# Second FFN GEMM of a transformer layer on plain float32 operands, with the query and key projections spread over more units

## The reference

```
q = x @ wq + x @ Aq @ Bq * 4;  k = x @ wk;  v = x @ wv + x @ Av @ Bv * 4      # heads of 16
q, k = rope(q), rope(k)
a = softmax(causal(q @ k.T / 4)) @ v;   x = layernorm(x + a @ wo)
h = gelu(butterfly(x @ W_exp + b_exp, up_weights) + up_bias)                  # 1024 wide
y = butterfly(h, down_weights) @ W_con + b_con + down_bias;   x = layernorm(x + y)
```

## Time and profile before

| | |
|---|---|
| median of 3 runs | 1371.78 us (1365.69 to 1373.66) |
| the profiled execution | 1372.62 us, its span 1370.9 us, mean granted clock of TensorE 0.923 |
| loop turns | begin about every 77 us |

### The profile page before, as it was taken

How to read it: one execution, slowest core, us unless ns; L and a number is a source line. 1 busy time by engine, 2 the same in 40 slices (tenths; PEclk the granted TensorE clock), 3 DMA queues, 4 the chain that set the end, 5 groups by cost and what they waited for, 6 DMA issues and landing times.

```text
span 1370.9 us, 27389 instructions
## 1 busy us (share of the span) xinstructions
PE 1154.4 (84%) x8328; PEld 811.3 (59%) x8328; DVE 834.9 (61%) x1896; ACT 757.5 (55%) x1259; POOL 630.8 (46%) x648
## 2 busy tenths in 40 slices
PE   4466789797889889898989899897989899899775
PEld 3334456665566566665666576665656576666464
DVE  5587766565647657475757667575757666575332
ACT  1156557465465657466564647466564647466612
POOL 2121424546355454637355454637355454635333
PEclk9667789999999999999999999999999999899999
DMA  5734454534445353544546353544546353542110
GB/s 184 191 119 111 132 125 112 150 102 140 105 147 139 118 148 94 169 118 135 118 147 144 114 148 94 167 119 135 118 147 146 112 148 94 170 117 60 49 40 31
DMA packets 94982, 169.88 MB, mean 124 GB/s; under 512 B 14872, under 2 KB 36120, under 8 KB 94944
## 3 DMA queue, kind: packets, MB, share of 16 engines
q1 hardware_dynamic: 93888, 166.53, 44.4%
q10 hardware_dynamic: 832, 1.83, 0.4%
q0 software_dynamic: 224, 1.04, 0.2%
HBM read 92.28 MB, written 77.07 MB: 124 GB/s over the span
## 4 chain that ended last, share of the span: by engine, by line
PE 53%; issue 14%; DVE 11%; POOL 11%; DMA 6%; ACT 4%; POOLq 0%; SPq 0%; DVEq 0%; ACTq 0%
PE ps_m L532 19%; PE ps_m L671 10%; PE ps_m L640 9%; PE ps_t L612 6%; POOL x1T_lo L1040 5%; DMA x_res<-in_x 4%; PE ps_s L574 3%; PE ps_s L600 3%; DVE m_raw L876 3%; POOL rot L1030 3%; DVE m_raw L871 2%; POOL pT L1020 2%; ACT pT L745 2%; DMA qk_scr<-rot 1%; PE ps_m L649 1%
## 5 line engine op out<-in xcount | busy, mean ns | idle before, releaser
L876 DVE TENSOR_REDUCE m_raw<-ps_s 128x1 f32<-128x512 f32 (+2 forms) x768 | 346.2, 506 | 278.8 <-PE ps_s L600 276.6
L745 ACT ACTIVATE pT<-ps_t 128x512 f32<-128x512 f32 x640 | 345.3, 593 | 148.4 <-PE ps_t L612 146.8
L1020 POOL TENSOR_SCALAR_AFFINE_SELECT pT<-pT 128x512 f32<-128x512 f32 (+1 forms) x320 | 175.4, 548 | 399.7 <-ACT pT L745 399.7
L1040 POOL TENSOR_TENSOR x1T_lo<-gact,x1T_hi 128x512 fp32r<-128x512 f32 x128 | 163.0, 1278 | 73.4 <-ACT x1T_hi L796 73.1
L574 PE MATMUL ps_s<-k_st,q_st 48*128 48x512 f32 (+3 forms) x1024 | 138.8, 329 | 43.9 <-DVE m_raw L876 22.6
L640 PE MATMUL ps_m<-pT,v_aug 128*32 128x512 f32 (+3 forms) x2048 | 170.8, 479 | 4.5 <-POOL pT L1020 3.3
L612 PE MATMUL ps_t<-q_st,k_st 50*128 50x512 f32 (+3 forms) x1024 | 173.0, 396 | 0.0
L671 PE MATMUL ps_m<-w_hi,x1T_hi 128*128 128x256 f32 x512 | 100.9, 324 | 67.4 <-POOL x1T_lo L1040 67.3
L612 PEld LDWEIGHTS ps_t<-q_st,k_st 50*128 50x128 f32 x1024 | 83.5, 190 | 90.2 <-issue 75.7
L574 PEld LDWEIGHTS ps_s<-k_st,q_st 48*128 48x128 f32 x1024 | 98.0, 195 | 56.3 <-DVE m_raw L876 32.2
L671 PEld LDWEIGHTS ps_m<-w_hi,x1T_hi 128*128 128x128 f32 x512 | 77.7, 212 | 77.8 <-POOL x1T_lo L1040 65.7
(11 more groups left out here) (119 smaller groups left out, 1984.7 us busy)
## 6 DMA issues: line engine op xcount, KB each, us to landing
qk_scr<-rot_hi SPq DMA_DIRECT2D x64, 512.0 KB, 3.6
q_st<-qk_scr SPq DMA_DIRECT2D x128, 192.0 KB, 4.7
k_st<-qk_scr SPq DMA_DIRECT2D x128, 192.0 KB, 5.1
qk_scr<-rot SPq DMA_DIRECT2D x32, 512.0 KB, 3.2
o_scr<-o_raw SPq DMA_DIRECT2D x64, 256.0 KB, 2.1
r_b<-in_xT SPq DMA_DIRECT2D x17, 512.0 KB, 6.5
o_c<-o_scr SPq DMA_DIRECT2D x32, 256.0 KB
r_b<-r_scr SPq DMA_DIRECT2D x32, 256.0 KB
```

The costliest lines, as they stand in the source:

```text
L745: act.activation(pT[:, g % 2, slot, half * T:(half + 1) * T], ps_t[:, ST_BANK[2 * n + r], :], ACT.Exp, scale=SCALE).then_inc(exp_done, 1)
L876: ins = dve.tensor_reduce(m_raw[:, r, u // 2, qt:qt + 1], ps_s[:, r, off:off + (qt + 1) * P], AX.X, ALU.max, negate=True)
L1020: pool.affine_select(out=v, in_=v, compare_op=ALU.is_ge, fill=0.0, base=0, pattern=pattern, channel_multiplier=-1).then_inc(mask_done, 1)
L1040: pool.tensor_tensor(g_lo[:, half, :, :], gact[:, NHT // 2 * half:NHT // 2 * (half + 1), tile * P:(tile + 1) * P], g_hi[:, half, :, :].bit ...
```

## The change

The second GEMM uses `gact` (the GELU's output) and one float32 `w2` as they are, with one product for each hidden tile in place of three matmuls. `w2_hi`, `w2_lo`, `g_hi`, `g_lo`, the steps GHI and GLO and their semaphores go; W2 waits for `gelu_done` of half 0, W2B for that of half 1, and DM writes `w2` only. `gact` is read by PE directly.

The tables change too. QK piece 0 of batch i+2 stands in unit 19's front, so behind S of unit 18, QK 1 of batch i+1 in unit 0, QK 2 in unit 2, QK 3 in unit 4. W1 pieces 6 and 7 move from unit 19 into units 0 and 1 of the next turn, and GE of half 1 from unit 0 to unit 1. W2 and W2B of tiles 0 and 1 stand together behind S of units 4 and 5, and tile 2 behind S of unit 6. RAW moves behind S of its unit, RB(i,0) ahead, XRES(i-1,0), LNS, HIGH, LOW, QKH and QKL later. The maxima's transpose MT is emptied by VectorE, no longer by ScalarE.

On PE, `QK3 MT1 | S10 PV3 | S11 W2-0 | S12 W2B-0 W2-1 | S13 W2B-1 | S14 W2-2 W2B-2 MT2` becomes `QK2 MT1 | S10 PV3 | S11 QK3 | S12 W2-0 W2B-0 | S13 W2-1 W2B-1 | S14 W2-2 W2B-2 MT2`. The diff, with the declarations left out:

```diff
@@ -67,15 +67,18 @@
 
 
 
-    qk, w2, wo, v, xt, w1 = i + 1, i - 2, i - 1, i + 1, i - 1, i - 1
-    front = {0: [("QK", qk, 0), ("QK", qk, 1)], 1: [("QK", qk, 2)], 2: [("QK", qk, 3), ("MT", i, 1)],
-             4: [("W2", w2, 0)], 5: [("W2", w2, 1)], 6: [("W2B", w2, 1)], 7: [("W2B", w2, 2), ("MT", i, 2)],
-             9: [("W2", w2, 3)], 10: [("WO", wo, 0)], 11: [("WO", wo, 1)], 12: [("V", v, 0), ("MT", i, 3)],
-             14: [("XT", xt, 0), ("XT", xt, 1)], 15: [("W1", w1, 0)], 16: [("W1", w1, 2)],
-             17: [("W1", w1, 4), ("MT", i + 1, 0)], 19: [("W1", w1, 6)],
-             3: [("PV", i - 1, 3)], 8: [("PV", i, 0)], 13: [("PV", i, 1)], 18: [("PV", i, 2)]}
-    back = {4: [("W2B", w2, 0)], 6: [("W2", w2, 2)], 9: [("W2B", w2, 3)], 14: [("V", v, 1)],
-            15: [("W1", w1, 1)], 16: [("W1", w1, 3)], 17: [("W1", w1, 5)], 19: [("W1", w1, 7)]}
+    front = {0: [("QK", i + 1, 1)], 1: [("W1", i - 2, 7)], 2: [("QK", i + 1, 2), ("MT", i, 1)],
+             3: [("PV", i - 1, 3)], 4: [("QK", i + 1, 3)], 5: [("W2B", i - 2, 0)], 6: [("W2B", i - 2, 1)],
+             7: [("W2B", i - 2, 2), ("MT", i, 2)], 8: [("PV", i, 0)], 9: [("W2", i - 2, 3)],
+             10: [("WO", i - 1, 0)], 11: [("WO", i - 1, 1)], 12: [("V", i + 1, 0), ("MT", i, 3)],
+             13: [("PV", i, 1)], 14: [("XT", i - 1, 0), ("XT", i - 1, 1)], 15: [("W1", i - 1, 0)],
+             16: [("W1", i - 1, 2)], 17: [("W1", i - 1, 4), ("MT", i + 1, 0)], 18: [("PV", i, 2)],
+             19: [("QK", i + 2, 0)]}
+    back = {0: [("W1", i - 2, 6)], 4: [("W2", i - 2, 0)], 5: [("W2", i - 2, 1)], 6: [("W2", i - 2, 2)],
+            9: [("W2B", i - 2, 3)], 14: [("V", i + 1, 1)], 15: [("W1", i - 1, 1)], 16: [("W1", i - 1, 3)],
+            17: [("W1", i - 1, 5)]}
+    if static and i == -1:
+        front[0] = [("QK", 0, 0), ("QK", 0, 1)]
     after = {"MT": "MOUT", "W2B": "W2E", "PV": "OE"}
 
     def gemms(table, t):
@@ -83,37 +86,27 @@
             put(kind, b, n)
             if kind in after:
                 put(after[kind], b, n)
-            if kind == "PV":
-                put("RAW", b, n)
-
-    def halves(b, n):
-        put("GHI", b, n)
-        put("GLO", b, n)
 
     for t in range(NU):
 
         if t == 0:
             put("FILL", i, 3)
-        if t == 2:
-            halves(i - 2, 0)
         for at, b, n in ((3, i, 1), (8, i, 2), (13, i, 3), (18, i + 1, 0)):
             if t == at:
                 put("MROW", b, n)
-        if t == 3:
-            halves(i - 2, 1)
         if t == 4:
             put("VC", i)
         if t == 5:
+            put("QKL", i + 1, 0)
             put("SMOC", i - 1, 1)
         if t == 6:
             put("RCP", i - 1, 1)
             put("REC", i - 1, 1)
         if t == 7:
-            put("XRES", i - 1, 0)
             put("RB", i - 1, 1)
-            put("LNS", i - 2, 2)
         if t == 8:
             put("ON", i - 1, 1)
+            put("LNS", i - 2, 2)
         if t == 10:
             put("LNS", i - 2, 3)
         if t == 12:
@@ -132,42 +125,38 @@
         if t == 17:
             put("LNB", i - 2, 2)
         if t == 18:
+            put("RB", i, 0)
             put("LNB", i - 2, 3)
 
         gemms(front, t)
-        for at, n in ((4, 2), (5, 4), (6, 5), (7, 7)):
-            if t == at:
-                halves(i - 2, n)
-        if t == 11:
-            put("LNS", i - 1, 0)
 
         put("ST", i, t)
         put("S", *((i, t + LEAD) if t + LEAD < NU else (i + 1, t + LEAD - NU)))
 
         gemms(back, t)
-        for at, n in ((4, 3), (6, 6)):
-            if t == at:
-                halves(i - 2, n)
 
         if t == 17:
             put("GE", i - 1, 0)
-        if t == 0:
+        if t == 1:
             put("GE", i - 2, 1)
         if t == 0:
             put("ROPE", i + 1, 0)
-        if t == 1:
+        if t == 2:
             put("HIGH", i + 1, 0)
+            put("LOW", i + 1, 0)
+        if t == 3:
             put("QKH", i + 1, 0)
-            put("LOW", i + 1, 0)
-        if t == 2:
-            put("QKL", i + 1, 0)
+        for at, b, n in ((3, i - 1, 3), (8, i, 0), (13, i, 1), (18, i, 2)):
+            if t == at:
+                put("RAW", b, n)
+        if t == 4:
             put("ROPE", i + 1, 1)
-        if t == 3:
+        if t == 6:
             put("HIGH", i + 1, 1)
             put("QKH", i + 1, 1)
-        if t == 5:
             put("LOW", i + 1, 1)
-        if t == 6:
+        if t == 7:
+            put("XRES", i - 1, 0)
             put("QKL", i + 1, 1)
         if t == 8:
             put("FILL", i + 1, 0)
@@ -184,7 +174,6 @@
         if t == 16:
             put("XLO", i + 2, 0, B + 1)
         if t == 18:
-            put("RB", i, 0)
             put("OUT", i - 2)
         if t == 19:
             put("ON", i, 0)
@@ -665,14 +649,12 @@
                 elif kind in ("W2", "W2B"):
 
                     half = int(kind == "W2B")
-                    pe.wait_ge(glo_done, NHT * b + 2 * n + half + 1)
-                    for j, (a, c) in enumerate(((0, 0), (0, 1), (1, 0))):
-                        for k in range(NHT // 2):
-                            mm = pe.matmul(pm[:, 0:D], (g_hi, g_lo)[a][:, half, k, :],
-                                           (w2_hi, w2_lo)[c][:, NHT // 2 * half + k, :],
-                                           start=(half + j + k == 0),
-                                           stop=(half == 1 and j == 2 and k == NHT // 2 - 1))
-                    mm.then_inc((w2_half, done["W2"])[half], 1)
+                    pe.wait_ge(gelu_done, 2 * b + half + 1)
+                    for k in range(NHT // 2 * half, NHT // 2 * (half + 1)):
+                        mm = pe.matmul(pm[:, 0:D], gact[:, k, n * P:(n + 1) * P], w2[:, k, :],
+                                       start=(k == 0), stop=(k == NHT - 1))
+                    if half:
+                        mm.then_inc(done["W2"], 1)
                 elif kind == "UM":
 
                     if n == 0:
@@ -785,17 +762,7 @@
                     act.activation(tile_up[n], pm[:, 0:D], ACT.Copy).then_inc(evac["UM"], 1)
                 elif kind == "DM":
                     act.wait_ge(done["DM"], n + 1)
-                    act.activation(w2_hi[:, n, :], pm[:, 0:D], ACT.Copy).then_inc(w2h_done, 1)
-                elif kind == "GHI":
-                    tile, half = n // 2, n % 2
-                    if tile:
-
-                        act.wait_ge((w2_half, done["W2"])[half], NT * b + tile)
-                    else:
-                        act.wait_ge(gelu_done, 2 * b + half + 1)
-                    act.activation(g_hi[:, half, :, :],
-                                   gact[:, NHT // 2 * half:NHT // 2 * (half + 1), tile * P:(tile + 1) * P],
-                                   ACT.Copy).then_inc(ghi_done, 1)
+                    act.activation(w2[:, n, :], pm[:, 0:D], ACT.Copy).then_inc(evac["DM"], 1)
                 elif kind in ("XU", "XD"):
 
                     k = int(kind == "XD")
@@ -894,6 +861,10 @@
                     dve.tensor_tensor(rope_in[:, a[0], :], pm, cs[:, a[1], :], ALU.mult)
                     dve.tensor_tensor(rope_in[:, c[0], :], pm, cs[:, c[1], :], ALU.mult)\
                        .then_inc(evac["QK"], 1)
+                elif kind == "MT":
+                    dve.wait_ge(done["MT"], NG * b + n + 1)
+                    wait(dve, mrow_out, DMA * (NG * b + n))
+                    dve.tensor_copy(m_row[:, :], pm[0:NM * GH * NT, 0:P]).then_inc(evac["MT"], 1)
                 elif kind == "XT":
                     dve.wait_ge(x1h_done, 2 * b + n + 1)
                     dve.tensor_tensor(x1T_lo[:, n, :], pm, x1T_hi[:, n, :].bitcast(FP32),
```

More of the change, by code:

```diff
@@ L178, in steps @@
         if t == 11:
+            put("LNS", i - 1, 0)
             put("XTL", i + 2, 0, B + 1)
@@ L279, in layer @@
             tmp_x = before_w2.enter_context(nc.sbuf_tensor("tmp_x", [P, 2, D], FP32))
-        w2_hi = sb("w2_hi", [P, NHT, D], F32R)
-        w2_lo = sb("w2_lo", [P, NHT, D], F32R)
+        w2 = sb("w2", [P, NHT, D])
         ga = gact[:, :, :].rearrange("p a c -> p (a c)")
@@ L346, in layer @@
         w_hi, w_lo = sem("w_hi"), sem("w_lo")
[L347 to L351, removed]
+        w1h_done = sem("w1_hi_done")
         pool_c = sem("pool_c")
@@ L763, in one @@
                        .then_inc(vcopy, 1)
[L764 to L768, removed]
                 elif kind == "HIGH":
@@ L917, in one @@
                        .then_inc(evac_w1[1], 1)
-                elif kind == "DM":
-                    dve.wait_ge(w2h_done, n + 1)
-                    dve.tensor_tensor(w2_lo[:, n, :], pm[:, 0:D], w2_hi[:, n, :].bitcast(FP32),
-                                      ALU.subtract).then_inc(evac["DM"], 1)
                 elif kind == "W2E":
@@ L1036, in one @@
                         .then_inc(on_done, 1)
-                elif kind == "GLO":
-                    tile, half = n // 2, n % 2
-                    pool.wait_ge(ghi_done, NHT * b + n + 1)
```

(5 more changed lines are left out.)

## The result

The changed kernel takes 1290.84 us (median of four executions, 1289.61 to 1295.52), the kernel before beside it on the same chip 1368.74 us (1365.09 to 1373.66). The ratio is 0.9435, 95% interval 0.9391 to 0.9479: 5.6% faster. The forecast of 1270 us was 21 us too low, inside its range. The profiled execution took 1295.52 us with a span of 1293.8 us, so 77 us of span are gone where the sum had 102.

What follows compares the result with a forecast made beforehand. PE's instruction stream was taken to set the turn: 77.0 - 9.2 + 1.9 + 0.65 = 70.3 us, taken as 70.0. 13 turns save 91 us, with start and end 102 us together: 1270 us, range 1243 to 1310.

Steps and rivals of the forecast that it cites:

- Part 1: GELU parts go: PE's GpSimd waits at the second GEMM and the slow stretch behind them vanish, 5.6 us a turn.
- Part 2: Second GEMM in plain float32: its eight halves cost PE 1.9 us more a turn, 2.5 at most.
- the walk: Step-by-step timing of a turn from S(i,6): WO starts at 39.1 us, before 46.2, so a turn of 69.9.
- Part 3: QK pieces set apart: at MT(i,1) 2.20 + 1.4 us of wait and slow stretch go, 0.65 come.
- Part 4: MT emptied by VectorE: three of four a turn cost nothing; unit 12's gains 0.1 us at most, none counted.
- the wait moves from MT3 to XT: Unit 12: MT(i,3) loses its 0.92 us wait, XT waits on VectorE's 0.3 us longer chain; gain 0.1 at most.
- Part 5: SP's queue reordered: maxima transfers and RB(i,0) earlier, XRES(i-1,0) and RB(i-1,1) later, at no cost, with 3.5 us of cover.
- Turns 15 and 16: W1 pieces 6 and 7 (3.0 us) fill PE's 3.25 us masks wait; plain halves cost 1.9; about 4 us gained.
- A: The waits move: about 2 us at MT1 or W2(i-2,0)'s bank plus slow stretch, 3.6 us a turn, 1317 us; chance 0.13.
- B: Slower: a wait ahead of unit 4 leaves GEMM 2 at half clock, up to 13.8 us a turn, 1449 us; chance 0.05.
- C: GEMM's waits pass to the next in line, 5.6 us a turn stay, 1343 us; chance 0.04, plus 0.02 shared with B.
- D: More gain: the 0.65 us, XT chain and three boundary waits vanish, 1.5 us a turn, 1250 us or under; chance 0.10.

Runs made afterwards that it cites:

- e7: The kernel before with only the second GEMM in plain float32, plus XRES(i-1,1) issued ahead of FILL(i+1,0): 1316.94 us, ratio 0.9603.
- e2: The kernel before, its own order of pieces kept, with only the second GEMM changed to plain float32: 1329.25 us, ratio 0.9709.
- e4: The changed kernel with MT emptied by ScalarE as before the change: 1287.16 us, ratio 0.9409.
- e10: e9 with MT emptied by ScalarE as before the change: 1260.79 us, ratio 0.9196.
- e9: e5 with the statistics LNS(i-1,0) moved to unit 10: 1263.08 us, ratio 0.9220.
- e1: The changed kernel with SP issuing XRES(i-1,1) ahead of FILL(i+1,0): 1268.91 us, ratio 0.9271.
- e5: The changed kernel with the rotation's stores (HIGH, QKH, LOW, QKL) issued earlier, FILL(i+1,0) left in place: 1266.24 us, ratio 0.9227.
- e11: e5 with half of GEMM 2's products left out, so the output is not the layer's: 1241.45 us, ratio 0.9069.
- e8: The changed kernel with half of GEMM 2's products left out, so the output is not the layer's: 1273.35 us, ratio 0.9315.

## Why the prediction was right or wrong

**Part 1, right.** No wait on the GELU's parts is left but 1.1 us in the last turn, and e7 gives the forecast's turn for the plain GEMM, 73.3 us.

**Part 2, right in size, and the rule did not decide.** Eight products are one group of 16 instructions in 3.46 to 3.67 us (665.84 above), 1.73 to 1.83 a half, 0.216 us an instruction. The estimate made with the Trainium skill ("FP8 and Floating Point Precision", TensorE Precision Notes: four passes for true FP32) was 1295 us, nearer to 1290.84 than the forecast. Its four passes agree with the trace, 0.432 us for a product, but its reason for the time isn't the one found. All eight halves of a turn stand ahead of WO, and there the walk holds: 39.4 us where 39.1 was forecast, so the 1.6 us a turn that the estimate adds aren't there. What is missing lies behind WO, and that it is 1.6 us a turn too is chance.

**Part 3, right.** MT1's wait went from 2.20 to 0.39 us, WO stands at 39.4 us, and in e2, which keeps the old order, MT1 still waits 2.2 us in every turn of the loop.

**Part 4, right in cost, wrong in what comes last.** e4 shows the cost of nothing, and e10 against e9 does so again. The step "the wait moves from MT3 to XT" failed: XT waits 0.32 us and MT3 1.79, because the sum ahead of `m_pad` waits for `x_res`.

**Part 5 is the step that failed.** It priced the steps that moved on SP's queue at nothing, with XRES(i-1,0) and RB among them. FILL(i+1,0) and XRES(i-1,1) did not move in the list, and I did not price them. But W2E(i-2,3), which releases the load, now comes 7 us sooner after S6, while the store of the keys' low half, which FILL needs, goes out only 2 us sooner (680.86 - 647.62 = 33.2 us after S6, before 721.36 - 686.21 = 35.2) and lands in 4.5 us instead of 3.1. The FILLs come 5 us sooner. So four FILL loads of 768 KB together, 2 us clear of the load before, now stand right ahead of it. It takes 1.5 us longer to land, and WO to XT gets 14.05 - 12.46 = 1.6 us longer a turn, 21 us in 13 turns. e1 and e5 take the cause away in two ways, and e5 has the turn that was forecast, 69.8. The four loads ahead are what slows it: e1 leaves the stores where they were, has FILL loads right behind the load and none right ahead, and there it lands in 2.9 to 3.2 us.

The prediction's opening says by the earlier trace rows that no DMA queue is near its limit; these rows have no DMA in them. The page has the busiest queue at 44.4% of its engines' time, which is a mean over the span and says nothing of these 2 us.

**Turns 15 and 16: 4 us of gain forecast, 7.4 lost.** Up to the last W1 they are 7.4 us longer, 6.8 of these up to the PV that the earlier trace rows show at 1297.29. The W1 pieces that moved across the boundary are 3.0 of the 6.8, and the plain GEMM 2.2. The pieces were to fit into a wait, but the waits up to that PV sum to 9.9 us, before to 10.0. About 2 us are W1 pieces that run at the lower clock behind waits: the first two matmuls of the one at 1204.38 take 1.19 us, before 0.70 in the same place. PV behind a wait takes 3.92 us in this turn, before 4.50, so PV isn't the difference. PE's timeline:

```profile
1153.13 0.80 PE L558 MATMUL ps_s<-k_st,q_st 48*128 48x384 f32 x4 [1.33 <-DVE m_raw L843]
...
1196.17 0.30 PE L616 MATMUL ps_m<-ident,m_pad 128*128 128x128 f32 x1 [1.78 <-DVE m_pad L854]
...
1196.82 3.92 PE L624 MATMUL ps_m<-pT,v_aug 128*32 128x512 f32 x32
...
1204.38 1.19 PE L516 MATMUL ps_m<-x1T_hi,w_hi 128*128 128x512 f32 x2 [1.62 <-DVE x1T_lo L870]
...
1224.88 3.97 PE L624 MATMUL ps_m<-pT,v_aug 128*32 128x512 f32 x32 [2.04 <-POOL pT L987]
```

The wait of 3.25 us into which the pieces were to fit became 2.04 us here, and the waits ahead of it grew by as much, from 6.8 to 7.8 us. I moved two pieces and did not walk these turns.

**The last turn, right.** From the last W1 to the end of the GEMM took 15.2 us, 5.3 less than before, forecast 5:

```profile
1270.65 1.89 PE L654 MATMUL ps_m<-w,gact 128*128 128x256 f32 x8
...
1273.66 12.35 PE L654 MATMUL ps_m<-w,gact 128*128 128x256 f32 x56 [1.12 <-ACT gact L795]
```

**Summed up.** Turns -1 to 1 gained 3.6 us (forecast 2), turns 2 to 14 gained 75.6 (91), turns 15 to the end lost 2.1 (9 gained): 77 of 102. The 13 turns sum to 932.5 us, before to 1008.1, where the forecast had 910 and 13 x 77.0 = 1001. The load's 21 us are in the 22 by which they are too long. But they had been 7 us longer than 1001 before (turn 3 took 81.6), and those hide a third of the load's share in the gain. So it is chance that the total was off by 21 us too, and that e1 and e5 come to 1269 and 1266 us, near the 1270 of the forecast: e5 gains some 9 us more in its 13 turns and 6 more ahead of them than was forecast, and loses 3 at the end where 9 were to be gained. **The rivals:** A had the right kind of event, a wait that takes the place of the one removed, but put it at MT1 or at W2(i-2,0), and priced it at 3.6 us a turn; it came at MT3 with 1.6. B did not come, the clock is 0.99. C is refuted by e7. D did not come.

**What stays open.** Whether PE alone would allow less than e10's time: e11 shows that a tenth less work gives 0.8 us a turn there, not what sets the rest.

## What to carry to other kernels

A step that keeps its place in the list can still change its neighbours in time: when an edit moves the release of one DMA and the data of another, write down for every load on the shared queue what has been issued in the 2 us ahead of it, and who waits for its landing. A busy share of 90% of the span, 96% of the loop, doesn't tell whether anything stands close behind the engine; taking a tenth of its work out (e8) tells it in one run, if the clock is read with it, since part of that work came back as slower matmuls. When a change has two parts, run each alone: here one is worth 39 us, the other -16, and both 78.

## What was not expected of the hardware

Removing 6.9 us of matmul a turn left the turn at 71.6 us, with TensorE busy 96% of the loop before: its clock fell from 0.99 to 0.94, and its busy time by 3.2 us only. A 256 KB load took 3.0, about 4.0 or 5.5 us, by what was issued ahead of it. The 16 KB store of the maxima, 1.4 us in the median, took 4.53 us in the turn shown, with two 512 KB stores of high parts issued 2.6 us ahead of it and that of the low parts 1.5 us behind.
